# The rows of the attention operand stacks are interleaved by head dimension, seven partitions apart, and each term of the product has a transfer of its own

## The reference

```python
def _L1_attn_ref(hidden_states, w_attn, b_attn, w_proj, b_proj):
    ...
    H, D = (NUM_HEADS, HEAD_DIM)            # 32, 16
    qkv = hidden_states @ w_attn + b_attn
    q, k, v = jnp.split(qkv, 3, axis=-1)
    ...
    scores = jnp.einsum('bqhd,bkhd->bhqk', q, k) * SCALE
    slopes = jnp.asarray(_alibi_slopes(H))
    rel = pos[None, :] - pos[:, None]
    bias = slopes[:, None, None] * rel[None, :, :]
    causal = rel <= 0
    scores = jnp.where(causal[None, None], scores + bias[None], -jnp.inf)
    attn = jax.nn.softmax(scores, axis=-1)
    out = jnp.einsum('bhqk,bkhd->bqhd', attn, v).reshape(B, S, HIDDEN)
    return out @ w_proj + b_proj
```

## Time and profile before

| | |
|---|---|
| median of 3 runs | 937.77 us (937.69 to 937.9) |
| the profiled execution's own time | 935.11 us |
| its span in the trace | 933.3 us |
| PE (TensorE) busy | 859.8 us, 92% |
| DVE (VectorE) busy | 759.0 us, 81% |
| ACT (ScalarE) busy | 437.8 us, 47% |
| POOL (GpSimd) busy | 264.5 us, 28% |
| chain that ended last | PE 60% of the span, DVE 6%, DMA 2% |

### The profile page before, as it was taken

How to read it: one execution, slowest core, us unless ns; L and a number is a source line. 1 busy time by engine, 2 the same in 40 slices (tenths; PEclk the granted TensorE clock), 3 DMA queues, 4 the chain that set the end, 5 groups by cost and what they waited for, 6 DMA issues and landing times.

```text
span 933.3 us, 12157 instructions
## 1 busy us (share of the span) xinstructions
PE 859.8 (92%) x4217; PEld 411.0 (44%) x4223; DVE 759.0 (81%) x1622; ACT 437.8 (47%) x798; POOL 264.5 (28%) x214
## 2 busy tenths in 40 slices
PE   6998868899989998699999999999999999999996
PEld 3434424354446444344444444444434444444442
DVE  5699999999998864689899989997245799776876
ACT  4777545656642121100666666667542656433100
POOL 1068999899974000040000000000000334000000
PEclk8989999999999999899999999999999999999998
DMA  9200060200005028410443144300014000000001
GB/s 349 93 0 1 1 270 22 113 1 0 1 4 198 0 75 181 126 64 4 84 79 64 17 77 79 70 11 2 1 62 181 0 0 1 0 1 0 12 34 45
DMA packets 21128, 54.33 MB, mean 58 GB/s; under 512 B 4950, under 2 KB 11734, under 8 KB 18059
## 3 DMA queue, kind: packets, MB, share of 16 engines
q1 hardware_dynamic: 14666, 47.26, 18.1%
q10 hardware_dynamic: 6400, 6.29, 2.2%
HBM read 44.96 MB, written 8.39 MB: 57 GB/s over the span
## 4 chain that ended last, share of the span: by engine, by line
PE 60%; DVE 6%; DMA 2%; issue 2%; POOL 1%; ACT 1%; ACTq 0%; POOLq 0%; DVEq 0%
PE ps L1185 16%; PE ps L1047 7%; PE ps L1196 6%; PE ps L1029 6%; PE ps L1069 4%; PE ps L1013 4%; PE ps L1016 3%; PE ps L1106 3%; PE ps L1086 3%; PE ps L958 2%; DMA parts_dram<-qkp 2%; PE ps L1032 2%; DVE ps L1455 1%; PE ps L952 1%; PE ps L771 1%
## 5 line engine op out<-in xcount | busy, mean ns | idle before, releaser
L724 ACT ACTIVATE prob<-ps 128x512 f32<-128x512 f32 x288 | 160.1, 599 | 125.9 <-PE ps L1032 97.6
L462 POOL TENSOR_TENSOR hC<-hs,C_sb 128x512 f32<-128x512 f32 x128 | 162.6, 1287 | 51.3 <-ACT C_sb L655 32.2
L938 PE MATMUL ps<-hC,identf 128*128 128x512 f32 x256 | 137.2, 638 | 22.3 <-POOL hC L462 21.0
L1029 PE MATMUL ps<-stack 123*128 123x512 bf16 (+3 forms) x384 | 113.8, 327 | 0.2
L586 ACT ACTIVATE ps<-dtT,nA 128x512 f32<-128x512 f32 x128 | 88.2, 690 | 48.9 <-DVE hs L1340 47.4
L418 POOL TENSOR_TENSOR rstd<-veps,mhalf 128x4 f32<-128x4 f32 x8 | 8.5, 1068 | 353.3 <-DVE veps L1223 353.3
L1462 DVE TENSOR_REDUCE mrow<-ps 128x1 f32<-128x512 f32 x128 | 81.9, 686 | 10.0 <-PE ps L1016 9.7
L938 PEld LDWEIGHTS ps<-hC,identf 128*128 128x128 f32 x256 | 44.4, 195 | 87.1 <-POOL hC L462 73.8
L1047 PE MATMUL ps<-prob,V 128*32 128x512 f32 (+3 forms) x768 | 81.6, 498 | 0.7 <-ACT prob L724 0.7
L1185 PE MATMUL ps<-hT,wg 128*128 128x512 f32 (+1 forms) x176 | 79.1, 592 | 0.0
L1185 PE MATMUL ps<-hT,wu 128*128 128x512 f32 (+1 forms) x176 | 79.1, 592 | 0.0
(11 more groups left out here) (199 smaller groups left out, 1331.6 us busy)
## 6 DMA issues: line engine op xcount, KB each, us to landing
wmod<-in_wmod SPq DMA_DIRECT2D x4, 1536.0 KB, 12.4
parts_dram<-qkp ACTq DMA_DIRECT2D x16, 384.0 KB, 2.6
stack<-parts_dram SPq DMA_DIRECT2D x16, 384.0 KB
wmod<-in_wmod SPq DMA_DIRECT2D x4, 1024.0 KB, 10.6
stack<-parts_dram SPq DMA_DIRECT2D x16, 256.0 KB
wattn<-in_wattn SPq DMA_DIRECT2D x1, 3072.0 KB, 11.2
wg<-in_wg SPq DMA_DIRECT2D x1, 2752.0 KB, 11.2
wu<-in_wu SPq DMA_DIRECT2D x1, 2752.0 KB, 9.4
```

Source lines behind the costliest of these rows:

```text
L462: pool.tensor_tensor(hC[:, c, :], hs[:, c, :], C_sb[:, m % 2, :], ALU.mult).then_inc(S["hc_done"], 1)
L724: A_(prob[:, u % 4, j, :], ps[:, 3 + F % 3, :], ACT.Exp).then_inc(S["exp_done"], 1)
L938: mm(ps[:, c, :], identf[:], hC[:, c, :], start=False, stop=(s == NS - 1), skip_group_check=True).then_inc(S["sum_done"], 1)
L1029: ins = mm(ps[:, bank, col:col + w], qk[0:ATT_ALL, 1, j, tile(kb)], qk[0:ATT_ALL, 0, j, q0:q0 + w], start=True, stop=not diag)
```

## The change

The rows of a stack are placed by d first: term n of dimension d stands on partition 7 d + n, for n = 0 to 5, and partition 7 d + 6 holds one of the first 16 rows of the positions. The other 8 rows of the positions stand on 112 to 119. The shift's rows stay on 120 to 122, so every matmul still contracts over 120 or 123 partitions. Each of the six terms has one transfer for q and one for k, each of 16 partitions with a step of 7. The rows of the positions need two transfers where they had one. A stack thus takes 14 transfers in place of 7, and a head's constants take three in place of two. The bytes are the same.

```diff
-ATT_K = 96
+TERMS = ((0, 0), (1, 0), (2, 0), (0, 1), (1, 1), (0, 2))
-ATT_S = ATT_K + ATT_A
+ATT_W = len(TERMS) + 1
+ATT_K = HD * ATT_W
+ATT_S = HD * len(TERMS) + ATT_A
+LOADS = 2 * len(TERMS) + 2
...
             def load_rows(s):
                 for j in range(GH):
-                    load(stack[s][ATT_K:ATT_S, 0, j, :].bitcast(U16), a["qconst"], S["in_att"])
+                    load(stack[s][ATT_W - 1:ATT_K:ATT_W, 0, j, :].bitcast(U16), a["qconst"][0:HD], S["in_att"])
+                    load(stack[s][ATT_K:ATT_S, 0, j, :].bitcast(U16), a["qconst"][HD:ATT_A], S["in_att"])
                     load(stack[s][ATT_S:ATT_ALL, 1, j, :].bitcast(U16), a["kones"], S["in_att"])
...
             def load_stack(g):
-                for first, count in ((0, 3), (3, 2), (5, 1)):
-                    at_ = g * GH * HD
-                    q = parts_dram[0:count, at_:at_ + GH * HD, :].rearrange("q (d h) t -> d q (h t)", h=GH)
-                    load(stack[g % 3][16 * first:16 * (first + count), 0, :, :], q, stk[g % 3])
-                    at_, part = D + g * GH * HD, 3 - count
-                    k = parts_dram[part:part + 1, at_:at_ + GH * HD, :].rearrange("q (d h) t -> d q (h t)", h=GH)                         .to_broadcast([HD, count, GH * T])
-                    load(stack[g % 3][16 * first:16 * (first + count), 1, :, :], k, stk[g % 3])
-                load(stack[g % 3][ATT_K:ATT_S, 1, :, :].bitcast(U16), a["alibi"][g], stk[g % 3])
+                def rows(part, first):
+                    at_ = first + g * GH * HD
+                    return parts_dram[part, at_:at_ + GH * HD, :].rearrange("(d h) t -> d (h t)", h=GH)
+
+                for n, (qp, kp) in enumerate(TERMS):
+                    load(stack[g % 3][n:ATT_K:ATT_W, 0, :, :], rows(qp, 0), stk[g % 3])
+                    load(stack[g % 3][n:ATT_K:ATT_W, 1, :, :], rows(kp, D), stk[g % 3])
+                load(stack[g % 3][ATT_W - 1:ATT_K:ATT_W, 1, :, :].bitcast(U16), a["alibi"][g][0:HD], stk[g % 3])
+                load(stack[g % 3][ATT_K:ATT_S, 1, :, :].bitcast(U16), a["alibi"][g][HD:ATT_A], stk[g % 3])
...
-                    pe.wait_ge(stk[g % 3], 16 * 7 * (g // 3 + 1))
+                    pe.wait_ge(stk[g % 3], 16 * LOADS * (g // 3 + 1))
                     if g == 2:
-                        pe.wait_ge(S["in_att"], 16 * (1 + 3 * 2 * GH))
+                        pe.wait_ge(S["in_att"], 16 * (1 + 3 * 3 * GH))
...
-                        pe.wait_ge(S["in_att"], 16 * (1 + 2 * 2 * GH))
+                        pe.wait_ge(S["in_att"], 16 * (1 + 2 * 3 * GH))
```

## The result

The changed kernel takes 925.87 us in the median (923.96 to 927.46, 4 runs), the kernel before, beside it, 937.84 us. The ratio is 0.9867 with a 95% interval of 0.9842 to 0.9892: 1.3% faster, 12.0 us. Forecast were 924.8 us. The profiled execution took 924.92 us (forecast 922.1), with a span of 923.1 us.

The account below looks back on a forecast made before the run. PE, busy 92%, was held by waits behind a late DRAM write and the low clock after them. The stretch from 366.42 to block 12 falls from 21.62 to 8.11 us; less 0.5, 937.8 - 13.0 = 924.8 us, range 923.3 to 932.

Parts of the forecast that it names:

- The cause: Stack loads in narrow bands fill the DMA engines; late write 6 delays negT, PE waits 7.77 us, then clocks low.
- The packets: DMA of one stack: 4.7 us of full engines at wu's rate, 10.6 us at the narrow loads' rate.
- The load of stack 0: SyncE's 14 issues, 6.4 us, plus 1.9 us landing: in at 363.6, at most 366.0; PE wants it at 366.42.
- The 2.61 us are gone: PE's wait for the last row of stack 0, 2.61 us, was to vanish, the load being covered by block 9.
- The sum: Mask matmul's end to block 12: 21.62 us becomes 8.11; gain at most 13.5, 13.0 us passed to the end.
- The constants: Four more load_rows transfers a stack, 1.4 us of issue, due some 70 us later: zero cost.
- The writes still lag: Rival, 0.19: write 6 lands about 370.5, negT 2.7 us late for PE; gain 8.4 us, 929.4 us.
- just full: Engines during the stack loads: 73% for stacks plus 30% for writes, so writes are not free of the loads.
- The band is not the reason: Rival, 0.12: 8 KB rows from parts_dram or repeated k rows are slow; engines full until 380, 937.8 us.
- Fixed time in turn: Rival, 0.05: each stack transfer costs 1.9 us in turn, 14 take 26.6 us; 4 us lost, 942 us.
- The signs: Profile: over 300 GB/s, idle after 371, later load 8 us, issues 0.46, blocks 3.65; wrong if stack 0 waits behind issues.

Follow-up runs that it names:

- e6: Kernel before, old layout and seven transfers, with one line moved: stack 1's load issued only after all 16 writes landed; 927.11 us, ratio 0.985 to 0.991.
- e1: Changed kernel's one transfer per term, but each term's 16 rows on neighbouring partitions, positions in a block of their own; 935.62 us, ratio 0.994 to 0.998.
- e2: Changed kernel with each term's 16 rows two partitions apart in a band of 32, positions in a block of their own; 926.36 us, one execution.
- e4: Changed kernel with the terms' rows six partitions apart over 0 to 95, positions in one transfer on 96 to 119; 927.22 us, ratio 0.985 to 0.990.
- e5: Changed kernel run again without edits, on the chip of the next three runs; 925.46 us, ratio 0.984 to 0.989.
- e9: e4 with q transfers ahead of k; groups 3 to 7 have own row steps and issue the first four q transfers one at a time; 931.01 us, one execution.
- e8: Changed kernel with pairs of terms interleaved in bands of 32 neighbouring partitions, eight transfers a stack; 926.02 us, ratio 0.985 to 0.991.
- e12: e4 with positions loaded early and the six q transfers of stacks 0 and 1 issued on GpSimd's queue; 928.92 us, one execution.
- e10: e8 with positions of groups 0 and 1 loaded early and stack 1 loaded after the writes; 924.36 us, ratio 0.983 to 0.988.
- e3: Changed kernel with four terms' rows four partitions apart over 0 to 63, two terms two apart over 64 to 95, positions separate; 925.31 us, one execution.

## Why the prediction was right, point by point

**The cause** held. The old stall was write 6 behind the stacks' packets (e6), and spreading the rows gives the engines room (e1 against e2 to e4). The wait for the write and the wait for negT went to zero, and blocks 10 and 11 went to 3.65 us each. The last of these holds some luck: the wait of 1.86 us that stayed left the clock at 1.00 in both executions profiled (the changed kernel and e5), while behind waits of 2.26 to 2.56 us for stack 0 in e9, e6 and e2 block 10 took 4.76 to 5.35 us.

**The packets** were mis-sized. I took 4.7 us of full engines a stack, the rate of wu; it was 6.2 us, inside the bounds of 4.7 and 10.6. With the writes beside them that made engines at a share of 0.94 while stack 0 was issued, and a landing that came later than I had it.

**The load of stack 0** was the step that failed, in both of its terms: the issues and the landing behind the last of them. For the issues I took 14 x 0.46 = 6.4 us and an upper bound of 8.8 us; from the first issue to the end of the last it was 9.57 us, over my bound. The single row of 0.42 us was of neighbouring partitions, as e1 shows, and the 0.59 us with a step is the price. Some issues were longer still (up to 0.88 us), so a median was no upper bound. For the landing I took 1.9 us, from a transfer of 8 KB; from the end of the last issue to step 0 it was 3.40 us. Together that is 12.97 us in place of 8.3, and PE wants stack 0 at 11.11 us after the first issue. "The 2.61 us are gone" was therefore wrong: 1.86 us of wait for stack 0 stayed. With the issues as measured and a landing of 1.9 us it would have been about 0.4 us, so most of it is the landing, behind engines that were not as free as I had them.

**The sum.** The 8.11 us for the stretch were 9.97 us; 8.11 + 1.86 = 9.97. The gain in the stretch was 11.65 us against the 13.0 that I passed to the end. The median moved by 12.0 us, inside the range, and 1.1 us from the forecast; that is within the jitter of the runs.

**The constants** cost nothing, as said: no wait in the profile names them. But their issues with a step took 0.50 us in the median and not 0.30, so the price had the same fault.

**The rivals.** *The writes still lag*: not in the changed kernel, where the longest took 5.0 us, but the forecast's "just full" was right in kind, since e8 and e12, which issue faster, have 5.37 and 6.7 us of such a wait. *The band is not the reason*: out by e1, in which the same cut transfers in narrow bands keep the engines full for more than 12 us. *Fixed time in turn*: out; e9 shows that one transfer at a time takes 2.5 us from issue to issue, so 14 in turn would take 35 us, and the changed kernel's fourteen were in within 12.97 us.

**The signs** came in part. No wait for parts_dram and blocks of 3.65 us were there. The twelve issues came at 0.63 us each and more, not 0.46. The engines' share was 0.88 from 357 to 376, but at 265 GB/s and not over 300; they were not idle soon after 371, since stack 1 was issued until 375.75; a later load took 11.7 us and not about 8. One sign of being wrong came true as well, the wait for stack 0.

**The rule against small transfers** in the Trainium skill, "DMA: Bandwidth & Descriptors", section "Rules for kernel authors", which wants them merged into a large one, would have spoken against this change. The trace does not follow it here: transfers of 128 KB with rows apart keep the engines full for 6.2 us, seven larger ones in narrow bands for 10.4 us. It has its point in the issues: fourteen take 9.57 us where seven took 4.40 us, and e10, with seven, is the one kernel without a wait for stack 0.

## What to carry to other kernels

When DMA engines are full but move little, look at which partitions the rows in flight go to; rows of 8 KB two or more partitions apart did here what a band of neighbours couldn't, and the real gain may lie with another queue's transfer that shares the engines. Before changing a layout, ask whether the load that fills the engines is due at all: moving the load of stack 1 behind the writes took one line and brought most of the gain. Price an issue by a row of the same addressing form, because a step between partitions made it 0.17 us dearer here, which is 2.4 us over fourteen. And price the landing behind the last issue by how full the engines are then: the row of an 8 KB transfer gave 1.9 us, and it was 3.4 us.

## What the runs showed that I had not expected

The issue of a transfer of 16 rows takes 0.42 us among others, 0.31 us alone, when its partitions are neighbours, and 0.59 and 0.50 us when there is a step of 2, 3, 4, 6 or 7 between them. What was issued just before counts too: the position load of 24 neighbouring rows takes 0.30 us among the constants (e10), 0.39 us behind a transfer of neighbouring rows (the kernel before) and 0.55 us behind one with a step (e2, e3, e4, e8). The slow issue may not be all loss: in e12 and e8, which issue a stack faster, a split waits 5 to 7 us for a write again. And e1, whose loads are the slowest of all, has a stretch 4.2 us shorter than the kernel before: its long wait for stack 0 and the first of its waits for writes lie on top of each other, where they followed one another before.

The same wait can cost the clock or not. In all fourteen profiled executions PE waits 2.12 or 2.13 us for V, 64 to 78 us behind the mask matmul. In four of them (e1, e5, e9, e10) the granted clock of the next 5 us is 0.66 to 0.68, in the other ten it is 1.00. The changed kernel and e5 are the same program:

```profile
434.29:439.29 5.00, 5.00 (x43) 2.65 (x44) 4.58 (x14) 3.77 (x7) 0.00 (x0) 1.00 0.22 64
```

```profile
433.76:438.76 5.00, 5.00 (x30) 3.04 (x31) 3.86 (x13) 3.00 (x6) 0.00 (x0) 0.66 0.24 66
```

e5 loses 1.6 us by it. The waits for stack 0 look alike: 2.26 us in e9 came before a block 10 of 5.35 us, 2.35 us in e4 before one of 3.65 us. Why it falls one way or the other, no run shows; a stretch of one execution can be off by 1 to 2 us for this alone.
